# GpSimd's diffusion and deviations requested one stage earlier in a transformer block with routed experts

## What is computed

```python
du   = zX * lap_x(x) + zY * lap_y(x) + zR * x * (1 - x)      # diffusion, per position
hn   = layernorm(du);   q, k, v = split(hn @ in_proj_w.T + in_proj_b)
attn = causal_softmax(q . k / 4) @ v                         # 16 heads of 16, over the 16 positions
x1   = du + attn @ out_proj_w.T + out_proj_b
hn2  = layernorm(x1);   top 2 of 8 experts per row from softmax(hn2 @ router_w.T)
y    = sum over the two experts of gate * (gelu(hn2 @ w1[e]) @ w2[e])
out  = x + x1 + y
```

## Time and profile before

| what | value |
|---|---|
| three runs | 807.04, 807.1 and 1448.99 us; median 807.1 us |
| profiled execution | 808.6 us, span 806.9 us, mean granted clock of TensorE 0.873 |
| busy over the span | PE 77%, DVE 55%, ACT 45%, POOL 54% |
| instructions | 9958 |

### The profile page before, as it was taken

One profiled execution on the slowest core, in us unless ns is written; L12 is line 12 of the kernel. 1 busy time (PEld: TensorE's weight loads), 2 busy tenths in 40 slices (PEclk: granted clock), 3 DMA queues, 4 the chain that ended last, 5 costly groups with the idle time before them and its releaser, 6 DMA issues.

```text
span 806.9 us, 9958 instructions
## 1 busy us (share of the span) xinstructions
PE 623.9 (77%) x2640; PEld 407.1 (50%) x2640; DVE 440.0 (55%) x1007; ACT 362.1 (45%) x822; POOL 436.4 (54%) x518
## 2 busy tenths in 40 slices
PE   1678884646556699599698987899889879999990
PEld 1234543433344566255365654567666556565660
DVE  1257999867999752358666785689932200011110
ACT  3444431314123447467466664456545535444430
POOL 4657744884485537565676547753373633333332
PEclk9778868668778889699799997989998989999995
DMA  3346552331121213232233223333243333333332
GB/s 99 102 158 202 182 176 69 100 108 27 26 76 44 40 34 87 59 62 53 59 101 56 56 53 61 69 45 45 46 91 61 89 58 61 61 55 62 57 47 26
DMA packets 51097, 59.81 MB, mean 74 GB/s; under 512 B 6938, under 2 KB 46627, under 8 KB 50980
## 3 DMA queue, kind: packets, MB, share of 16 engines
q0 software_dynamic: 18288, 23.28, 18.0%
q1 hardware_dynamic: 32756, 35.90, 14.9%
HBM read 35.89 MB, written 27.46 MB: 79 GB/s over the span
## 4 chain that ended last, share of the span: by engine, by line
DMA 26%; POOL 25%; DVE 18%; PE 15%; issue 11%; ACT 3%; SPq 1%; POOLq 0%; DVEq 0%; ACTq 0%
DMA out_dram<-y,xin 23%; POOL xs_d L386 7%; DVE qk_prod L791 5%; DVE sc L799 4%; PE b_y L933 3%; PE b_qk L1010 3%; POOL rstd L378 3%; PE b_h L918 3%; DMA xud<-in_x_dram 3%; POOL out_dram L412 2%; POOL du L371 2%; POOL rstd L377 2%; DVE pv_prod L862 2%; POOL xud L362 2%; POOL du L372 2%
## 5 line engine op out<-in xcount | busy, mean ns | idle before, releaser
L412 POOL DMA_INDIRECT out_dram<-y,xin x71 | 115.1, 1621 | 165.4 <-DMA out_dram<-y,xin 129.8
L918 PE MATMUL b_h<-w_s,xT 128*128 x284 | 139.2, 614 | 6.9 <-ACT xT L468 6.9
L933 PE MATMUL b_y<-w_s,hm_hmT 128*128 x568 | 137.8, 386 | 5.2 <-ACT hm_hmT L497 4.2
L933 PEld LDWEIGHTS b_y<-w_s,hm_hmT 128*128 128x128 f32 x568 | 104.7, 194 | 18.0 <-issue 6.3
L791 DVE TENSOR_TENSOR qk_prod<-q,kv 128x1024 f32<-128x1024 f32 (+2 forms) x80 | 92.9, 1163 | 11.5 <-ACT kv L537 11.1
L1054 PE MATMUL b_at<-ident,pv_prod 128*128 128x128 f32 x544 | 81.5, 303 | 21.8 <-DVE pv_prod L862 21.8
L862 DVE TENSOR_TENSOR pv_prod<-kv,pr 128x1024 f32<-128x1024 f32 (+2 forms) x80 | 91.6, 1188 | 12.3 <-PE b_at L1054 12.0
L377 POOL TENSOR_SCALAR rstd<-mv 128x1 f32<-128x1 f32 x64 | 27.0, 422 | 131.0 <-DVE mv L778 102.9
L642 DVE TENSOR_SCALAR y<-b_y,xin,live 128x256 f32<-128x256 f32 x22 | 12.0, 544 | 144.7 <-PE b_y L933 141.3
L1054 PEld LDWEIGHTS b_at<-ident,pv_prod 128*128 128x128 f32 x544 | 72.1, 162 | 27.1 <-issue 24.3
L1010 PE MATMUL b_qk<-wqkv,hT 128*128 128x512 f32 x128 | 83.6, 788 | 0.0
(11 more groups left out here) (160 smaller groups left out, 1011.7 us busy)
## 6 DMA issues: line engine op xcount, KB each, us to landing
xin<-xs_d SPq DMA_DIRECT2D x71, 132.5 KB, 2.1
w_s<-in_L_ffn_w_dram SPq DMA_DIRECT2D x16, 512.0 KB, 7.7
xp<-in_x_dram SPq DMA_DIRECT2D x32, 128.0 KB
xud<-in_x_dram SPq DMA_DIRECT2D x32, 128.0 KB
out_dram<-x POOLq DMA_DIRECT2D x32, 128.0 KB, 3.3
xud<-in_x_dram SPq DMA_DIRECT2D x32, 127.0 KB
out_dram<-y,xin POOLq DMA_INDIRECT x71
xs_d<-ring,slot_row POOLq DMA_INDIRECT x64
```

What stands on the lines that cost most here:

```text
L412: pool.indirect_dma_start(out_rows, bass.IndirectOffsetOnAxis(ap=xin[:, j % NX, H:H + 1].bitcast(U32), axis=0), y[:, j % NY, :], None, com ...
L918: mm = pe.matmul(b_h[:, :], xT[:, k * P:(k + 1) * P], w1_s[:, bass.ds(e * (HC * F) + k * F, F)], start=(k == 0), stop=(k == HC - 1))
L933: mm = pe.matmul(b_y[:, 0:H], hmT[:, k * P:(k + 1) * P], w2_s[:, bass.ds(e * (FC * H) + k * H, H)], start=(k == 0), stop=(k == FC - 1))
```

## The change

- GpSimd's loop begins one iteration earlier (`AHEAD = 4`), and its order is new: the first of the finished tiles is added, then `diffuse(g + 4)`, a scatter, `neighbours(g + 5)`, then `deviation(g + 3, 0)`, the second finished tile's `add_y`, `deviation(g - 2, 1)`, `add_x1(g - 2)` and the second scatter. ACT's `scale` and SP's `load` follow: step g + 4 and step g + 5.
- DVE takes the statistics of `du` for step g + 3 behind `x1`, in the middle of iteration g. Both normalisations stand at the head of the next iteration: `ring` for step g - 3, `hn` for step g + 2.
- Buffers: `du` 7 instead of 6, `x1` 4 instead of 2 (with 4 semaphores `x1_added`), `mv` and `rstd` two each.
- Routing is one iteration later (`ROUTE` + 4), top-2 selection is always that of step g - 4, two scatter steps an iteration (`PER = 2`) instead of three. `ENDS` has 27 for 28: the last group has 5 steps instead of 4.
- `WANT` is as before, but no group is scattered early enough for iteration 15 any more: slots 0 and 1 stand in iteration 16, and so on, up to slot 32 in iteration 34. The tail begins two tiles earlier, and it scatters 5 steps instead of 4.

```diff
-    ENDS = (5, 9, 13, 18, 23, 28, G)
+    ENDS = (5, 9, 13, 18, 23, 27, G)
...
-    DU = 6
+    DU = 7
+    AHEAD = 4
...
-        ROUTE = {GROUPS[r][-1] + 3: r for r in range(NG - 1)}
-        PER = 3
+        ROUTE = {GROUPS[r][-1] + 4: r for r in range(NG - 1)}
+        PER = 2
...
-            for g in range(-3, G + 3):
-                if 2 <= g + 4 < G:
-                    load(g + 4)
+            for g in range(-AHEAD, G + 3):
+                if 2 <= g + AHEAD + 1 < G:
+                    load(g + AHEAD + 1)
...
-            for g in range(-3, G + 3):
-                if 0 <= g + 2 < G:
-                    deviation(g + 2, 0)
-                for j in done_in(g - 1):
-                    add_y(j - 1)
+            neighbours(0)
+            for g in range(-AHEAD, G + 3):
+                adds = [j - 1 for j in done_in(g - 1)]
+                for j in adds[:1]:
+                    add_y(j)
+                if g + AHEAD < G:
+                    diffuse(g + AHEAD)
+                if g == -AHEAD:
+                    later_constants()
                 scatter_at(g, 0)
-                if g + 3 < G:
-                    neighbours(g + 3)
-                scatter_at(g, 1)
+                if g + AHEAD + 1 < G:
+                    neighbours(g + AHEAD + 1)
+                if 0 <= g + 3 < G:
+                    deviation(g + 3, 0)
+                for j in adds[1:]:
+                    add_y(j)
                 if 0 <= g - 2 < G:
                     deviation(g - 2, 1)
                     add_x1(g - 2)
-                if g + 3 < G:
-                    diffuse(g + 3)
                 if g == list(ROUTE)[0] + 3:
                     prefix()
-                scatter_at(g, 2)
+                scatter_at(g, 1)
...
+                if 0 <= g - 3 < G:
+                    unit(x1[:, (g - 3) % 4, :], g - 3, 1)
+                if 0 <= g + 2 < G:
+                    unit(du[:, (g + 2) % DU, :], g + 2, 0)
                 if 0 <= g < G:
...
-                        if m == 0 and g + 2 < G:
-                            st = stats()
...
-                if 0 <= g + 2 < G:
-                    unit(du[:, (g + 2) % DU, :], g + 2, 0)
+                first = stats() if 0 <= g + 3 < G else None
...
-                if 0 <= g - 2 < G:
-                    unit(x1[:, g % 2, :], g - 2, 1)
```

More of the change, by code:

```diff
@@ L103, in adaln_moe_block @@
         pr = sb("pr", [P, 2, NH * S])
-        x1 = sb("x1", [P, 2, H])
+        x1 = sb("x1", [P, 4, H])
         small = sb("small", [P, 64])
@@ L109, in adaln_moe_block @@
         junk = sb("junk", [P, 2])
-        mv = sb("mv", [P, 2, 2])
-        rstd = sb("rstd", [P, 3])
+        mv = sb("mv", [P, 2, 2, 2])
+        rstd = sb("rstd", [P, 2, 2])
+        power = sb("power", [P, 1])
         logits = sb("logits", [P, G, E])
@@ L145, in adaln_moe_block @@
         s = {n: sem(n) for n in names}
-        x_in, x1_added = [pair(n) for n in ("x_in", "x1_added")]
+        x_in = pair("x_in")
+        x1_added = [sem(f"x1_added{i}") for i in range(4)]
         xin_in = [sem(f"xin_in{i}") for i in range(NX)]
@@ L189, in scattered_by @@
             return max([g for (g, n), step in SCATTER.items() if step == GROUPS[r][-1]] + [G + 3 if r == NG - 1 else 0])
-        SLOTS = {(g, n): [] for g in range(-3, G + 3) for n in range(NPLACES)}
+        SLOTS = {(g, n): [] for g in range(-AHEAD, G + 3) for n in range(NPLACES)}
         at = -1
@@ L315, in _ @@
                 sp.wait_ge(copied[i], 16)
-            for i in range(2):
-                sp.wait_ge(x1_added[i], 16 * (G // 2))
+            for i in range(4):
+                sp.wait_ge(x1_added[i], 16 * (G // 4))
             sp.wait_ge(s["y_added"], 16 * ALL)
@@ L401, in add_x1 @@
                     pool.wait_ge(copied[p // (S // NCOPY)], 16)
-                pool.dma_start(out[p, c * P:(c + 1) * P, :], x1[:, g % 2, :], accum_op=ALU.add).then_inc(x1_added[g % 2], 16)
+                pool.dma_start(out[p, c * P:(c + 1) * P, :], x1[:, g % 4, :], accum_op=ALU.add).then_inc(x1_added[g % 4], 16)
             def add_y(j):
@@ L407, in add_y @@
                 if j in FIRST:
-                    for i in range(2):
-                        pool.wait_ge(x1_added[i], 16 * len([g for g in range(ENDS[group_of(j)]) if g % 2 == i]))
+                    for i in range(4):
+                        pool.wait_ge(x1_added[i], 16 * len([g for g in range(ENDS[group_of(j)]) if g % 4 == i]))
                 if j >= 1:
@@ L569, in _ @@
                     odds(ROUTE[g - 1])
-                if 0 < g + 3 < G and not diffused_late(g):
-                    scale(g + 3)
+                if 0 < g + AHEAD < G and not diffused_late(g):
+                    scale(g + AHEAD)
                 if g >= 0 and SLOTS[g, 0] and g < G:
@@ L588, in _ @@
                 place(g, 1)
-                if 0 < g + 3 < G and diffused_late(g):
-                    scale(g + 3)
+                if 0 < g + AHEAD < G and diffused_late(g):
+                    scale(g + AHEAD)
                 if g - 3 >= 0:
@@ L804, in _ @@
                         multiply(m)
-                        if m == 0 and g + 2 < G:
-                            st = stats()
                         if m >= 1:
                             add_up(m - 1)
-                        if m == 1 and g + 2 < G:
-                            aggregate(st)
-                            aggregated = True
                     add_up(NPIECE[g] - 1)
-                if 0 <= g + 2 < G and not aggregated:
-                    aggregate(st if g >= 0 else stats())
                 if 0 <= g < G:
@@ L847, in _ @@
                     total = tick(dve.reciprocal(small[:, 32:32 + NH], small[:, 16:16 + NH]))
-                    ordered = top(g - 4) if 0 <= g - 4 and g - 1 not in ROUTE else None
+                    ordered = top(g - 4) if 0 <= g - 4 else None
                     need(total)
@@ L851, in _ @@
                     if ordered:
-                        top_index(ordered)
+                        last = top_index(ordered)
                     need(total)
@@ L870, in _ @@
                     need(st)
-                    dve.wait_ge(s["xhat2"], g - 2)
-                    dve.bn_aggr(mv[:, 1, :], small[:, 54:60]).then_inc(s["stats2"], 1)
-                if 0 <= g - 2 < G:
-                    unit(x1[:, g % 2, :], g - 2, 1)
-                for step in ([g - 4, g - 3] if g == G + 1 else [g - 3] if g in ROUTE or g > G + 1 else []):
+                    dve.wait_ge(s["xhat2"], g - 3)
+                    dve.bn_aggr(mv[:, 1, g % 2, :], small[:, 54:60]).then_inc(s["stats2"], 1)
+                for step in ([g - 4, g - 3] if g == G + 1 else [g - 3] if g > G + 1 else []):
                     last = top_index(top(step))
```

43 lines of the change are left out of this document (23 added, 20 removed).

## The result

| | time |
|---|---|
| kernel before | 807.8 us (median) |
| changed kernel | 875.2 us (median; 873.6 to 875.9) |
| ratio | 1.0835, 95% interval 1.0811 to 1.0859 |
| forecast | 781 us, range 762 to 807 |

The account below looks back on a forecast made before the run. The prediction found no single engine bounding the run and read it by stage. From the 807.1 us median, terms of +4, -16, -15.5, -26, +5, +11 and +11.5 summed to -26: 781 us, range 762 to 807.

Parts of the forecast that it names:

- Prologue and first iterations, +4: Up to iteration 8: first scores 13 us later, then 7.5 and 2 us come back; about +4 us.
- lower bound of -2: Best case of the prologue term: -2 us, if loads land faster once the weights do not share the queue.
- Iterations 9 to 16, -16: Iterations 9 to 16: `rstd` and `du` ready an iteration early, DVE's work unchanged; 140 us against 156.4, -16 us.
- PE's iterations 18 to 22 and 23 to 29, -15.5 and -26: PE sets the pace once the stall is gone: 13.5 us per one-tile iteration, 16.9 per two-tile; -15.5 and -26 us.
- The three signs by which the forecast was to fail: First scores later than 55 us, PE waiting for `xin` in the loop, GpSimd never waiting for `stats1` in iterations 18 to 29.
- GpSimd's own load, +5: Iterations with two adds and two scatter steps take GpSimd about 17.5 us, just over PE's 16.9; +5 us.
- Routing ahead of `ring`, +11: PE waits for `ring` behind `route_b` for the groups routed in iterations 22, 27 and 31; +11 us.
- Tail, +11.5: End of the run: two more adds at 4.45 us and two more scatter DMAs at 1.3 us; +11.5 us.
- The rivals: Whole-run alternatives: about 762 us (chance 0.12), 798 (0.17 with mixed cases), 811 (0.08), 840 (0.11 with anything else above 823).
- the slower one: Iterations 23 to 33: late second add makes PE wait some 5 us per tile; about 840 us, 0.11 with others above 823.
- rival 2: GpSimd and VectorE bound together, diffusions meeting DVE's products (+10) and GpSimd's order (+7); about 798 us, 0.17 with mixed cases.

Follow-up runs that it names:

- split_load: ring_first with the 127-row copy in every load of x issued as two copies, of 112 and 15 rows; 753.3 us, ratio 0.9366.
- scale_head: The changed kernel with ACT's scale of step g + 4 moved to the head of its iteration g; 787.4 us, ratio 0.9749.
- scale_early: The changed kernel with ACT's scale of step g + 4 behind the exponentials in all iterations; 786.3 us, ratio 0.9733.
- ring_first: scale_head with DVE writing `ring` ahead of `route_b` again in the iterations that have one; 774.0 us, ratio 0.9570.
- before_two_late: The kernel before with no expert tile in iteration 15, so two more tiles stand in the tail; 814.5 us, ratio 1.0081.
- diffuse_last_three: The changed kernel with GpSimd's diffusion back behind the deviations and the add of x1, and three load buffers instead of two; 803.0 us, ratio 0.9966.
- three_loads: scale_head with three buffers for the loads of x instead of two; 787.1 us, ratio 0.9719.

## Why the prediction was wrong

By its own steps.

- **Prologue and first iterations, +4: mis-sized.** The +13 up to the first subtraction was right (+13.5), the 9.5 us given back afterwards were not (+15.2 at the ninth). The step assumed that two iterations cost one load and one round of GpSimd, 8.3 us each. The first five cost 10.1 each (47.4 to 97.8), and the next three 37.3 us instead of 34.6. The load is not all of that pace: in split_load, where GpSimd never waits for one, the same five still take 47.8 us, 9.6 each. The chain of waits runs between PE and ACT there (PE's queries, keys and values, then ACT's `hT`, scale and `aT`, then PE again), and ACT waits 28.4 us of the 47.8 for PE's values; the step had neither engine in its loop. What the slow load did cost is nearly all ahead of the first subtraction, 12.9 of the 14.6 us that split_load has gained by the ninth. The prediction called the nearly 8 us of the arrival long for 128 KB and took it as given; with the copy of 127 rows split, the load's 8.7 us became at most 5.0. Its lower bound of -2, by loads that land faster without the weights, was an estimate that no run shows: in the kernel before the DMA share reads 0.07 at 24 GB/s behind a load's issues in the prologue (24 to 27), and the same long after the weights (460 to 463).
- **Iterations 9 to 16, -16: right** (-18.2).
- **PE's iterations 18 to 22 and 23 to 29, -15.5 and -26: this failed.** The sentence was "With the stall gone PE sets the pace". The stall was not gone. I followed GpSimd's wait on `stats1`, which the diff shows, and priced GpSimd's own load, but not the wait of the instruction that the change had put first: `diffuse(g + 4)` waits for ACT's scale, and I never looked where ACT does it. The order of GpSimd of both kernels, shown with the change, has "waits scaled" on that row, at the end before and at the head after. In place of the 13.5 and 16.9 us an iteration the runs showed a turn of 20.7 to 29.0 us as long as there is a diffusion, that is up to iteration 27 (+27.4 and +24.5). scale_head and scale_early, which only move the scale, have the iterations about as forecast (69.2 and 71.7 us for 18 to 22, 123.5 and 124.9 for 23 to 29). The three signs by which the forecast was to fail would not have caught it: the first scores came at 47, PE waited for `xin` once in these iterations (1.0 us), and GpSimd was seen waiting for `stats1` once (2.9 us).
- **GpSimd's own load, +5: not shown apart.** Iterations 23 to 29 of scale_head took 5.2 us more than 118.3, of which 2.5 are the wait behind a `route_b`, so it was 2.7 at most there; in 18 to 22 nothing of it is to be seen (69.2 less the 4.9 behind a `route_b` is under 67.5).
- **Routing ahead of `ring`, +11: right**, 13.4 by ring_first. In the changed kernel itself only the 4.9 us at PE's iteration 32, behind the last of the late scales, can be read apart from the loop.
- **Tail, +11.5: too large**, +5.9 in the trace, and in before_two_late the two tiles alone cost +6.0 where the step has 8.9. The adds (8.8) and the scatters (2.7) are there, and 5.6 us ahead of them came back, as 4.5 did in before_two_late's loop; the step counted what the tail takes and not what comes back ahead of it. Its count of 35 intervals of 4.45 us was 34 of 4.58, which changes the term by 0.3 us.
- **The rivals.** All four missed, and the slower one named the wrong wait: the second add behind `stats1` starved nothing (PE waits at most 1.0 us for a tile in these iterations). For rival 2, the middle addition of the diffusion has its median at 0.72 us in the changed kernel against 1.19, so this cost fell instead of rising. The meetings themselves are in the trace of before: at 147.08 the addition took 1.60 us beside a product of DVE's from 146.12 that took 1.97, while the next product of the same size, at 149.85 and without it, took 1.21. The long waits are not the reason: it is 0.73 in scale_head too, where they are nearly gone, and 1.56 in diffuse_last_three, where the diffusion stands last. Whether the fall comes from fewer such meetings was not tested.

Put together, the forecast of 781 was near the kernel that I had in mind, which is the changed one with the scale early: 786 to 787. Part of that nearness is luck: in scale_head the start is 10 us dearer than forecast (+14.3 at the ninth), while the tail (+7.9 for +11.5) and iterations 18 to 22 (69.2 for 73.5) are 8 us cheaper.

## What to carry to other kernels

When an instruction moves to the head of an in-order engine's row, its own wait moves with it: follow that semaphore to the engine that posts it, find the place of the post in that engine's row, and go on until the loop closes or leaves the iteration; the loop inside one iteration cost the sum of all its parts here, 20.7 us in the turn shown, with PE busy 13.8 us an iteration. An experiment that moves an instruction also moves whatever its end releases (a load's buffer here), so read the waits of each experiment before taking its time as a verdict. And a load that arrives late for its bytes deserves a look at its shape before it gets another buffer: 112 and 15 rows beat 127 by 17 to 21 us, and a third buffer did nothing.

## What was not expected of the hardware

- A DMA's issue was held for microseconds behind the copy ahead of it: SP's last issue of a load, right behind the copy of 127 rows, had a median of 2.6 us in the changed kernel and 6.0 in three_loads (8.0 in the row shown), and 0.4 us where that copy was split, and everything behind it in SP's row waited.
- In the iterations in which PE waited it was also busy for longer. The same 256 matmuls kept it busy 69.1 us in iterations with 6 to 11 us of wait at their start (mean granted clock 0.75), 63.5 us in the kernel before (0.84), and 58.4 us in scale_head, where only two of these waits are above 0.9 us (3.4 and 4.9) and the clock reads 0.97. These means are made of two readings, 0.50 and 1.00 of full speed; no trace here has a third, so 0.75 is about half the time at 0.50. In the kernel before it reads 0.50 from 328.9 to 342.6, around the end of the 8.9 us wait of the earlier trace rows, and 1.00 from 342.6 to 352.0; in iteration 21 it reads 0.62 from 365.5 to 369.8 and 1.00 from 369.9 to 379.4.
